# Two MoE runs with expert products in three fp32r terms, and the last run's down products too

## What is computed

```python
# layer 0: E, K, H = 8, 2, 176; layer 1: 32 experts, top 6, F_EXP = 96
logits = x @ gate_w
scores = jax.nn.softmax(logits, axis=-1)
topk_w, topk_idx = jax.lax.top_k(scores, K)
...
g = jax.nn.silu(jnp.einsum('td,edh->teh', x, w_gate)) * jnp.einsum('td,edh->teh', x, w_up)
routed = jnp.einsum('teh,ehd,te->td', g, w_down, comb)
shared = jax.nn.silu(x @ sw_gate) * (x @ sw_up) @ sw_down
out = (routed + shared).reshape(b, s, d)
```

## Time and profile before

| | |
|---|---|
| median of 3 runs | 1366.76 us |
| the three runs | 1365.97, 1366.76, 1370.21 us |
| profiled execution, its own time | 1363.16 us |
| its span | 1361.3 us |
| granted TensorE clock, mean over the span | 0.914 |
| PE busy | 1136.8 us (84%) |
| DVE busy | 753.1 us (55%) |
| ACT busy | 487.6 us (36%) |
| POOL busy | 583.4 us (43%) |

### The profile page before, as it was taken

The page is one execution under the profiler, slowest core; times in us unless marked ns, Lnnn a source line. Parts: engine busy times, 40 slices in busy tenths (PEclk is TensorE's granted clock), DMA queues, the critical chain, the costliest instruction groups (busy, mean ns, idle before and its releaser), DMA issues.

```text
span 1361.3 us, 19456 instructions
## 1 busy us (share of the span) xinstructions
PE 1136.8 (84%) x5926; PEld 924.3 (68%) x5926; DVE 753.1 (55%) x2317; ACT 487.6 (36%) x936; POOL 583.4 (43%) x571
## 2 busy tenths in 40 slices
PE   4999996688898998997465599999988584999993
PEld 3776774456677886775353499998564563999993
DVE  5763365636455653366524184767777542656665
ACT  3422343374454422343231144444242311444441
POOL 3670243221112221227777302667507776006675
PEclk9899998898898999998577799999998687999997
DMA  9622435910000047743322567887302223568986
GB/s 326 262 71 84 142 104 189 334 37 1 0 1 32 32 179 270 256 136 126 126 100 94 192 187 218 276 265 236 106 1 93 98 97 115 161 191 272 283 278 203
DMA packets 125154, 210.03 MB, mean 154 GB/s; under 512 B 15280, under 2 KB 104752, under 8 KB 123184
## 3 DMA queue, kind: packets, MB, share of 16 engines
q1 hardware_dynamic: 100480, 141.64, 31.2%
q0 software_dynamic: 24576, 67.14, 15.6%
HBM read 129.56 MB, written 101.19 MB: 170 GB/s over the span
## 4 chain that ended last, share of the span: by engine, by line
PE 56%; POOL 12%; DVE 12%; issue 10%; ACT 5%; DMA 4%; SPq 0%; ACTq 0%; POOLq 0%; DVEq 0%
PE ps L828 16%; PE ps L838 11%; POOL xd L588 10%; PE ps L746 5%; PE ps L799 5%; PE ps L758 4%; PE ps L1105 3%; PE ps L809 3%; PE ps L971 2%; POOL G L602 2%; PE ps L978 2%; ACT xnt L1213 2%; DMA G<-yd,slot_of 1%; PE ps L887 1%; DMA yd<-yo 1%
## 5 line engine op out<-in xcount | busy, mean ns | idle before, releaser
L602 POOL DMA_INDIRECT G<-yd,slot_of x256 | 249.6, 975 | 356.4 <-DMA yd<-yo 255.4
L588 POOL DMA_INDIRECT xd<-xnt,slot_of x256 | 254.7, 995 | 185.9 <-DVE slot_of L1754 102.0
L828 PE MATMUL ps<-WE,xT 128*128 x1016 | 190.3, 331 | 0.3
L1348 ACT ACTIVATE xT<-ps 128x512 f32<-128x512 f32 (+1 forms) x168 | 99.3, 591 | 213.8 <-PE ps L799 213.6
L1864 DVE TENSOR_TENSOR hid<-hid,ps 128x192 f32<-128x192 f32 (+2 forms) x168 | 65.4, 389 | 183.9 <-ACT hid L1367 183.2
L828 PEld LDWEIGHTS ps<-WE,xT 128*128 128x128 f32 x1016 | 165.7, 194 | 1.1 <-issue 0.9
L1843 DVE SCALAR_TENSOR_TENSOR XT<-G,wt,XT 128x256 f32<-128x256 f32 x256 | 124.7, 488 | 45.0 <-DMA G<-yd,slot_of 32.8
L1871 DVE COPY yo<-ps 128x512 f32<-128x512 f32 (+1 forms) x168 | 114.8, 684 | 61.3 <-PE ps L838 61.3
L799 PE MATMUL ps<-ident,xd_in 128*128 128x128 f32 x664 | 103.4, 278 | 37.4 <-DMA xd_in<-xd 31.3
L838 PE MATMUL ps<-WE,hT 96*128 x508 | 130.8, 380 | 0.0
L1232 ACT ACTIVATE S<-ps 128x512 f32<-128x512 f32 (+1 forms) x72 | 42.8, 595 | 242.0 <-PE ps L746 237.4
(11 more groups left out here) (225 smaller groups left out, 1886.8 us busy)
## 6 DMA issues: line engine op xcount, KB each, us to landing
xd_in<-xd SPq DMA_DIRECT2D x164, 256.0 KB, 3.9
yd<-yo SPq DMA_DIRECT2D x164, 256.0 KB, 3.0
WE<-w SPq DMA_DIRECT2D x8, 1280.0 KB, 6.8
W0E<-w0e SPq DMA_DIRECT2D x2, 4864.0 KB, 24.1
xd<-xnt,slot_of POOLq DMA_INDIRECT x256, 2.4
G<-yd,slot_of POOLq DMA_INDIRECT x256, 3.9
XT<-x_in SPq DMA_DIRECT2D x4, 512.0 KB, 5.8
out<-XT SPq DMA_DIRECT2D x16, 128.0 KB, 3.4
```

The costliest lines, as they stand in the source:

```text
L588: nc.gpsimd.indirect_dma_start(xd[f // 2][:, :], bass.IndirectOffsetOnAxis(ap=slot_of[:, t, k:k + 1], axis=0), xnt[:, t, :], None).then_in ...
L602: nc.gpsimd.indirect_dma_start(G[:, n % G_RING, :], None, yd[f // 2][0:min(ly.early[t] * 2, ly.TILES) * P, :], bass.IndirectOffsetOnAxis(a ...
L828: last = mm(dst, xT[:, q % 2, a, k, :], flat[:, bass.ds(expert[2 * q + a] + k * 2 * ly.H, 2 * ly.H)], start=(k == 0), stop=(k == KD - 1))
L1348: fn(xT[:, q % 2, 0:m].rearrange("p a k t -> p (a k t)"), ps[:, TX, 0:m * D], ACT.Copy).then_inc(TL.xT, 1)
```

## The change

In runs 0 and 1 (`HALVED`) the rows and the gated rows are split as in the shared chunks (`x_low`, `h_low`), and each fp32 product is three fp32r products. ACT makes the high parts of the experts' weights (`expert_high`), POOL the low parts (`expert_low`, eight subtractions of 128x1216 for each run: behind the scatters of run 0, and between the scatters of blocks 2 and 3 of run 1). The down products follow two pairs behind in all runs and use two banks in turn. In runs 0, 1 and 3 ACT copies the finished rows (`finished`). In run 3 the down products are three fp32r terms too: ACT and DVE split the down weights in four parts (`down_high`, `down_low`), DVE subtracts the low part of the gated rows (`h_low3`), and PE reads a second register for the place of the high weights. The up products of run 3 and all of run 2 stay in fp32. The loads and splits of the channel weights go behind the products of run 0 (`channel_weights`); the second load of layer 0's expert weights is issued earlier, most of layer 1's after run 1's last rows. The buffers of several arrays move.

```diff
@@ SP
-            for i in range(SPLIT0, SPLIT1):
-                sp.dma_start(raw_wa[i - SPLIT0][:, :], pieces[i][0]).then_inc(wa_in, 16)
-            sp.dma_start(WSQ[:], wsq).then_inc(wsq_in, 16)
+            sp.dma_start(WSQ[:, 0:4 * SQW], wsq[:, 0:4 * SQW]).then_inc(wsq_in, 16)
...
-                behind = 6 if f < 2 else 7
+                behind = 7
...
             tiles(0)
+            sp.wait_ge(TL.down, PAIR0[1])
+            for i in range(SPLIT0, SPLIT1):
+                sp.dma_start(raw_wa[i - SPLIT0][:, :], pieces[i][0]).then_inc(wa_in, 16)
...
             sp.wait_ge(CK.gu, RUN["c", 3][0][-1].i + 1)
-            sp.wait_ge(CK.gu, RUN["s", 1, 1][0][-1].i + 1)
-            sp.wait_ge(F_NORM[1].lo, 2)
-            sp.wait_ge(RT.logits, 4 + 2)
             sp.wait_ge(A0.crm, NB)
             sp.dma_start(W0E[:], w0e).then_inc(w0e_in, 16)
@@ POOL
             for b in range(NB):
                 scatter(0, b)
-            pool.wait_ge(wa_in, 16 * HID)
-            for i in range(SPLIT0, SPLIT1):
-                _, dst, start, n = pieces[i]
-                split(i, raw_wa[i - SPLIT0][:, :], dst, start, n)
-            pool.wait_ge(w_ready, SPLIT1)
+            def expert_low(l, e):
+                pool.wait_ge(ew_hi, LY[0].E * l + e + 1)
+                nc.gpsimd.tensor_tensor(W0L[:, e, :], W0E[:, e, :], W0H[:, e, :].bitcast(F32), ALU.subtract).then_inc(ew_lo, 1)
+
+            for e in range(LY[0].E):
+                expert_low(0, e)
...
             inverse(F_NORM[1], NB - 1)
-            for b in range(STAGES - 4, NB):
-                scatter(1, b)
+            scatter(1, NB - 2)
+            for e in range(LY[0].E):
+                expert_low(1, e)
+            scatter(1, NB - 1)
@@ PE, up
+                    if f in HALVED:
+                        pe.wait_ge(TL.xlo, q + 1)
+                        for a in range(ly.tiles_in(i)):
+                            for k in range(KD):
+                                at = bass.ds(expert[2 * q + a] + k * 2 * ly.H, 2 * ly.H)
+                                dst = ps[:, bank + a, 0:2 * ly.H]
+                                mm(dst, xTh[:, q % 2, a, k, :], flat_hi[:, at], start=(k == 0), stop=False)
+                                mm(dst, xTh[:, q % 2, a, k, :], flat_lo[:, at], start=False, stop=False)
+                                last = mm(dst, xTl[f][:, q % 2, a, k, :], flat_hi[:, at], start=False, stop=(k == KD - 1))
@@ PE, order in tiles
-                    if f < 2:
-                        if q > q0:
-                            hturned(q - 1)
-                        if ahead:
-                            ahead(q - q0)
-                        up(q)
-                        if between:
-                            between(q - q0)
-                        if q > q0:
-                            down_rows(q - 1)
...
+                    if ahead:
+                        ahead(q - q0)
+                    up(q)
+                    if q > q0:
+                        hturned(q - 1)
+                    if q > q0 + 1:
+                        down_rows(q - 2)
+                    if between:
+                        between(q - q0)
@@ ACT
+                def finished(q):
+                    act.wait_ge(TL.down, q + 1)
+                    if q >= Y_RING:
+                        act.wait_ge(TL.sent[q % Y_RING], 16 * (q // Y_RING))
+                    m = ly.tiles_in(q - q0)
+                    fn(yo[:, q % Y_RING, 0:m].rearrange("p a d -> p (a d)"), ps[:, down_bank(f, q), 0:m * D], ACT.Copy).then_inc(TL.y, 1)
...
+                    if (f in HALVED or f == 3) and q > q0 + 1:
+                        finished(q - 2)
@@ DVE
+                if f in HALVED:
+                    x_low(q0)
                 for q in range(q0, q1):
+                    if f in HALVED:
+                        if q + 1 < q1:
+                            x_low(q + 1)
+                    gated(q)
+                    if f in HALVED and q > q0:
+                        h_low(q - 1)
                     if ahead:
                         ahead(q - q0)
-                    gated(q)
                     if between:
                         between(q - q0)
-                    if q >= q0 + lag:
+                    if f == 3:
+                        if q > q0:
+                            h_low3(q - 1)
+                    elif f not in HALVED and q >= q0 + lag:
                         rows(q - lag)
```

More of the change, by code:

```diff
@@ L29 @@
 LAG = 2
+HALVED = (0, 1)
 class Layer:
@@ L536, in _ @@
                 sp.dma_start(stage1[:, c, :], wsh1[c]).then_inc(sh1_in, 16)
+            for g in range(2, 7):
+                expert_group(g)
             def attention_weights(i):
@@ L631, in _ @@
                     inverse_lead(1)
+            for h in range(3):
+                channel_weights(h)
             for s in range(1, STAGES):
@@ L1893, in tiles @@
                         beside(q - q0)
-                for q in range(q1 - lag, q1):
-                    rows(q)
+                if f == 3:
+                    h_low3(q1 - 1)
+                elif f in HALVED:
+                    h_low(q1 - 1)
+                else:
+                    for q in range(q1 - lag, q1):
+                        rows(q)
                 return done[0]
```

301 lines of the change are left out of this document (223 added, 78 removed).

## The result

The changed kernel takes **1395.26 us** (median of 4 runs, 1395.18 to 1395.53); the kernel before took 1367.39 beside it (4 runs, 1365.97 to 1370.21). The ratio is 1.0205, with an interval of 1.0183 to 1.0228: 28 us slower, outside the predicted range of 1334 to 1371 and on the side that had 0.22.

The account below looks back on a forecast made before the run. No engine bounds the whole: PE bounds the first and last runs' products, POOL's chain the second run's later half. 3 - 7.6 + 3 + 7.6 - 7.9 - 9.4 = -11.3 us, from 1366.8 to 1355.5; range 1334 to 1371.

Parts of the forecast that it names:

- What a pair costs: Expert products: a layer-0 pair falls from 4.98 to 4.23 us, 0.75 less; a last-run pair, at 2.83, takes 0.15 less.
- Rival C: Expert products bound by PE instructions: pairs take 4.5 us in layer 0, 2.8 in the last run; 1373 us; chance 0.10.
- Start, +3: Before run 0's first products: POOL's weight subtractions slow DVE's low halves, 2.6 us plus 0.4; bounds 0 and +3.3.
- Drain, +7.6, upper bound +12.9: End of run 1's preparation: POOL's weight subtractions delay DVE's choice of experts, +7.2 and +0.4 us; bounds +3.4 and +12.9.
- Run 0's products, -7.6: Run 0's expert products: fifteen pairs save 11.3 us; DVE's statistics cost 0.6 and the tail to the keys 3.1.
- Mixing, +3: Mixing after run 0: POOL's splits of the channel weights slow DVE's serial chain by 3 us; bounds 0 and +6.
- Run 1, -7.9: Run 1's products: pairs 0 to 10 save 8.3 us, less 0.4 for the first; pairs 11 to 17 save nothing.
- Last run, -9.4: Last run's down products as fp32r terms: 0.15 us less per pair over 63 pairs, 9.4 us saved.
- Splitting its down weights, 0, up to +4 if it doesn't hide: Last run's shared chunks: ACT's and DVE's weight splits hide beneath POOL's scatters, costing 0, or up to 4 us.
- B: POOL's splits lock DVE out at drain, mixing and start: about 24 us of holds, 1366 to 1372 us; chance 0.15.
- A: PE's saving in the expert products arrives whole: 39 us less, 1327 us, or 1345 half-way; chance 0.22.

Follow-up runs that it names:

- e4: Changed kernel with VectorE adding run 0's gathered rows of tiles 8 and later one pair later: 1390.90 us, ratio 1.0178.
- e7: Changed kernel with e4's later gathers, and ScalarE doing the mixing's rows and keys ahead of its copy of finished rows in run 0: 1386.82 us, ratio 1.0144.
- e11: Changed kernel with layer 0's low weights on DVE, e7's order, and the last run's low down weights from PSUM in e10's steps: 1357.53 us, ratio 0.9937.
- e6: Changed kernel with the low parts of run 3's down weights subtracted from PSUM, where PE puts the high parts: 1404.94 us, ratio 1.0289.
- e10: Kernel before plus run 3's part alone, high down weights passed through PSUM in sixteen fp32r steps between shared-chunk parts: 1357.57 us, ratio 0.9940.
- e3: Changed kernel with run 3's down products and rows put back as in the kernel before: 1394.86 us, ratio 1.0220.
- e2: Changed kernel with each of POOL's sixteen 1216-column subtractions cut into four of 304 columns, back to back: 1399.89 us, ratio 1.0244.

## Why the prediction was wrong, step by step

- *What a pair costs*: right. 4.23 forecast and 4.24 measured in layer 0 (151.64 to 155.88), 2.68 in the last run (1250.76 to 1253.44) against 2.67 forecast. Rival C, with 4.5 and 2.8, is refuted.
- *Start, +3*: **the step that failed.** The sum put the wait of DVE's low halves (512 columns, two SBUF inputs) beside POOL's subtractions at 2.6 us here, with 3.3 as the bound, and at 0.4 in the drain, where only the upper bound had DVE wait for all of POOL's work. POOL ran five and then six operations without a gap, and the low half waited for the train's end: +12.9.
- *Drain, +7.6, upper bound +12.9*: same step, +17.1. The low half ahead of the choice of experts, priced at 0.4, waited 13.2. The three small groups, priced at 7.2 with one POOL operation each, fared as assumed or better: two of their operations were held, by one POOL operation each, 1.6 and 2.5. The upper bound let DVE through at 508, 22 us behind the third group's last scatter (486.1); it was 26.2 (507.4 to 533.6), because the last two subtractions came 4.2 us later, behind ACT's high parts, and held the choice of experts again. The place was right: DVE rows of over 2 us, and PE's last rank ahead of the scatters, at 534.28, 26.9 us behind the third group's end where the forecast had 19.
- *Run 0's products, -7.6*: +4.9, 12.5 off, more than either of those two. The fifteen pairs up to 185.51 gave 9.8 of the 10.7 that the sum has for them. The tail, put at +3.1 with +6 as its bound, cost 14.7. e4 and e7 show two thirds of it (9.6) to be order: gathers and mixing steps ahead of `xTl` on DVE, the finished rows ahead of the mixing's rows on ACT. How much of the rest is the lower clock behind PE's waits was not taken apart.
- *Mixing, +3*: +3.5, right in size. But e11, which has no weight subtraction of layer 0's experts on POOL, has +4.6 here, so it belongs to the moved channel weights or to something else there; that stays open.
- *Run 1, -7.9*: -6.4, near in size; its terms were not read one by one.
- *Last run, -9.4*: -8.3. *Splitting its down weights, 0, up to +4 if it doesn't hide*: +8.8. DVE's subtractions of 2048 columns hold POOL's scatters, a direction of the hold that I hadn't considered; e6 and e10 show it by its absence. With e3, which has none of these subtractions, the stretch still takes 3.3 us more than before (131.1 against 127.8).
- *The rivals*: B had the mechanism and the sign, and its threshold (25 us of holds) was passed: 12.9 + 17.3 + 6.9 = 37.1. It gave 1366 to 1372, since it took the bounds of the same sum. A would have needed the saving to reach the end; e11 shows that without POOL's weight subtractions it doesn't.

I had one row of a hold, 1.85 us of DVE beside 1.89 of POOL, and read from it that a hold is one operation long. POOL's timeline of the kernel before goes on, without a gap:

```profile
399.50 2.93 POOL L652 TENSOR_TENSOR XT<-XT,XA 128x1024 f32<-128x1024 f32 x1
```

So DVE's 4 columns did get in at the boundary of a train there, and the reading holds for an operation of that size. It was carried over to 512 columns, for which the row showed nothing.

The Trainium skill, page "SBUF — State Buffer", section "Who interferes with whom", has it that a VectorE instruction with two SBUF inputs contends with a GpSimd instruction that reads SBUF, and, of VectorE's two-port modes, that whoever issues first gets the shared pair for the whole instruction and the other is blocked. The traces agree in the lock. That it ends with the instruction they bear out for the small operations (1.81 us, and 0.75 and 0.87 in e2) and not for those of 512 columns: 11.43 and 13.90 us beside instructions of 2.8.

## What to carry to other kernels

Before two-input elementwise work goes to GpSimd, look at what VectorE has there with two inputs in SBUF and price the hold at the whole back-to-back train, not at one operation, wherever VectorE has rows of hundreds of columns; keep such trains away from serial chains, or put a gap between their operations. VectorE's large two-input operations in turn belong away from GpSimd's indirect DMAs, unless one input comes from PSUM. And a saving on an engine that is at 100% in one stretch must be followed to the end: here the pairs of two runs saved 0.75 us each, and the work around them gave all of it back in the usual jobs.

## What the runs showed of the hardware

- GpSimd's lock on a VectorE subtraction of 512 columns can span a train of operations: 11.43, 13.90 and, with pieces of a quarter, 13.53 and 16.44 us, each ending 0.55 after the train. VectorE operations of 4 to 32 columns get in at the next boundary (1.85, 1.81, 0.75 us), and so did one of 512 columns in e2 (0.88 us at 101.41). With a one-input operation and a semaphore wait between GpSimd's long ones, 3.07 us is the most.
- What it holds: two inputs in SBUF, and also the one-input TENSOR_SCALAR on 128x32 that took 1.81 us at 529.08, where the shortest of its line takes 0.17. With one input in PSUM: 0.69, not held.
- VectorE's subtraction of 128x2048 with both inputs in SBUF holds GpSimd's indirect DMA instruction: 2.31 to 3.00 us instead of 0.97, four of four. It isn't the length alone: beside subtractions of 1.22 us with one input in PSUM six scatters take 0.97 or 0.98 (e6), and one beside an operation of 1.22 us with both inputs in SBUF takes 1.93 (at 775.93 in the changed kernel). The Trainium skill's section named above says that a `tensor_tensor` was not seen to stall DMA, and takes as inferred that it leaves descriptor generation alone. The rows show the instruction lengthened; whether its reading of the slots or its writing of descriptors is held they don't show.
- The difference of two tensors costs GpSimd twice what it costs VectorE: 2.8 and 1.40 us for 128x1216.
